# Token routing of a two-FFN transformer block: paired token sums, statistics three batches ahead, a new order on ScalarE

## The reference, cut to what matters

```python
x = x + 0.5 * ffn(layernorm(x))          # first FFN
x = x + attn(layernorm(x))
x = x + 0.5 * ffn(layernorm(x))          # second FFN
# in ffn, per batch, S = 64 slots:
h = gelu(concat(x, slot_mean) @ w1 + b1)                  # 128 hidden
route_logits = (h @ w2 + b2) / (abs(tau) + 0.1)           # 64 logits a token
topk_vals, topk_idx = top_k(route_logits, 8)
alpha = scatter(softmax(topk_vals))                       # weights, zero off the top 8
slot_input = einsum('bts,btd->bsd', alpha, x)
si = slot_input / (alpha.sum(axis=1) + 1e-8)
# then a GRU cell, slot attention, layernorm, and out = alpha @ slot_values @ wo + bo
```

## Time and profile before

| what | value |
|---|---|
| time, median of 3 runs (lowest, highest) | 3647.28 us (3645.79, 3649.57) |
| the profiled execution | 3644.44 us |
| its span | 3642.4 us |
| mean granted TensorE clock | 0.973 |
| busy: PE / DVE / ACT / POOL | 94% / 84% / 75% / 28% |
| routing, first FFN | 17.88 to 239.1 us |
| routing, second FFN | 3274.7 to 3495.5 us |

### The profile page before, as it was taken

How to read it: one execution, slowest core, us unless ns; L and a number is a source line. 1 busy time by engine, 2 the same in 40 slices (tenths; PEclk the granted TensorE clock), 3 DMA queues, 4 the chain that set the end, 5 groups by cost and what they waited for, 6 DMA issues and landing times. The chain is left out here.

```text
span 3642.4 us, 60476 instructions
## 1 busy us (share of the span) xinstructions
PE 3420.0 (94%) x22538; PEld 1210.3 (33%) x22538; DVE 3065.4 (84%) x4480; ACT 2722.1 (75%) x5316; POOL 1023.3 (28%) x835
## 2 busy tenths in 40 slices
PE   6998489999999999999999999999999999958987
PEld 4644212232322323232323232323232232215653
DVE  6965499999999999999999999999999989808965
ACT  4740158888888888888888888888888888856730
POOL 2320323232323232333333342323232321212310
PEclk8999679999999999999999999999999999988999
DMA  3225302121212121121212121112121212112217
GB/s 103 93 94 214 141 22 54 43 54 43 54 43 62 43 57 43 54 60 41 64 43 60 41 63 44 54 42 54 43 60 44 59 31 54 40 52 77 93 71 300
DMA packets 123093, 246.53 MB, mean 68 GB/s; under 512 B 34657, under 2 KB 75425, under 8 KB 108465
## 3 DMA queue, kind: packets, MB, share of 16 engines
q1 hardware_dynamic: 115712, 208.06, 20.5%
q10 hardware_dynamic: 7088, 34.61, 2.3%
HBM read 121.91 MB, written 51.38 MB: 48 GB/s over the span
## 5 line engine op out<-in xcount | busy, mean ns | idle before, releaser
L1360 DVE TENSOR_REDUCE attn_part_max<-attn_ps 128x2 f32<-128x1024 f32 x2048 | 2447.3, 1221 | 244.7 <-PE attn_ps L1500 202.7
L1625 ACT ACTIVATE attn_probs<-attn_ps 128x512 f32<-128x512 f32 x4096 | 2171.1, 600 | 363.1 <-PE attn_ps L1512 362.7
L1512 PE MATMUL attn_ps<-attn_q_rows,attn_k_rows 50*128 50x512 f16 x4096 | 1273.0, 384 | 29.4 <-ACT attn_probs L1625 16.1
L1500 PE MATMUL attn_ps<-attn_k_rows,attn_q_rows 48*128 48x512 f16 x4096 | 1140.2, 388 | 30.2 <-DVE attn_part_max L1360 26.6
L1526 PE MATMUL attn_ps<-attn_probs,attn_v_ones 128*32 128x512 f32 x8192 | 1091.8, 605 | 0.7 <-ACT attn_probs L1625 0.7
L1512 PEld LDWEIGHTS attn_ps<-attn_q_rows,attn_k_rows 50*128 50x128 f16 x4096 | 307.3, 94 | 1324.8 <-ACT attn_probs L1625 1249.6
L1500 PEld LDWEIGHTS attn_ps<-attn_k_rows,attn_q_rows 48*128 48x128 f16 x4096 | 225.4, 94 | 174.0 <-DVE attn_part_max L1360 159.4
L1526 PEld LDWEIGHTS attn_ps<-attn_probs,attn_v_ones 128*32 128x32 f32 x8192 | 161.1, 108 | 237.4 <-issue 136.8
L1452 PE MATMUL attn_ps<-attn_xn_parts,attn_w_qk 128*128 128x256 f16 x1536 | 214.3, 278 | 6.2 <-POOL attn_xn_parts L1284 6.2
L1247 POOL CAST attn_max_parts<-attn_max_whole 32x128 f16<-32x128 f32 x64 | 17.9, 279 | 687.8 <-ACT attn_max_whole L1577 666.6
L1272 POOL TENSOR_TENSOR attn_xn_t<-attn_o_packed,attn_inv_wide 128x1024 f32<-128x1024 f32 x32 | 75.4, 2357 | 397.5 <-DMA attn_inv_wide<-inverse_denominators 397.5
(11 more groups left out here) (170 smaller groups left out, 2649.7 us busy)
## 6 DMA issues: line engine op xcount, KB each, us to landing
attn_q_rows<-attn_parts SPq DMA_DIRECT2D x384, 64.0 KB, 2.2
attn_k_rows<-attn_parts SPq DMA_DIRECT2D x384, 64.0 KB, 2.2
ffn_x_ring<-in_L_attn_x SPq DMA_DIRECT2D x16, 1024.0 KB, 5.7
attn_x_ln<-after_first_ffn SPq DMA_DIRECT2D x16, 1024.0 KB, 4.8
attn_o_packed<-attn_o_sb SPq DMA_DIRECT2D x256, 64.0 KB, 2.3
attn_inv_wide<-inverse_denominators SPq DMA_DIRECT2D x32, 512.0 KB
attn_x_res<-after_first_ffn SPq DMA_DIRECT2D x16, 1024.0 KB, 5.1
after_attention<-attn_x_res SPq DMA_DIRECT2D x16, 1024.0 KB, 8.6
```

Source lines behind the costliest of these rows:

```text
L1360: dve.tensor_reduce(part_max[:, G % 2, :, j, t, half], pair, AX.X, ALU.max).then_inc(dve_emptied, 1)
L1500: last = pe.matmul(ps[:, bank + e, :], q_rows[rows_e, G % NG, j, t * P:(t + 1) * P], k_rows[rows_e, G % NG, j, half * HALF:(half + 1) * HA ...
L1512: pe.matmul(ps[:, bank, :], k_rows[rows_e, G % NG, h // 2, kt * P:(kt + 1) * P], q_rows[rows_e, G % NG, h // 2, half * HALF:(half + 1) * H ...
L1625: act.activation(probs[:, quad % NQ, h, :], bank_of(s, b0), ACT.Exp, scale=1.0 / (SCALE * SCALE)).then_inc(act_emptied, 1)
```

## The change

Only the routing block is changed.

- The ring has 8 places. SyncE loads eight batches at once, and batch b from 8 on once pair (b-8)//2 has been summed.
- `sum_tokens` works on a pair of batches: in each step four token tiles, for each tile the even batch and right behind it the odd one. A pair is summed in the steps 2p+3 (tiles 0 to 3) and 2p+4 (tiles 4 to 7).
- TensorE's step n is now `hidden(n)`, fills 0 and 1 of batch n+1, `logits(n)`, fills 2 and 3 of batch n+1, `turn_sums` (odd steps), half of a pair's sums, `turn_weights` (odd steps).
- VectorE's step n is `find_top(n)`, `normalise(n+2)`, `statistics(n+3)`, `weigh(n)`, and `divide` in even steps. The shift is no longer made by VectorE: it makes the negated mean, and GpSimd multiplies it with rstd right behind `rsqrt`.
- The total of the eight weights comes from eight extra columns: GpSimd appends the top 8 logits less the largest to `shifted`, Exp takes 72 columns a tile instead of 64, and VectorE adds up 8 of them instead of the 64 picked ones.
- ScalarE's step n is Exp of batch n-1, Gelu of n, fills 0 and 1 of n+1, then in even steps `normalise(n+2)`, fills 2 and 3, `alpha_t`, in odd steps fills 2 and 3, `si_t`, `normalise(n+2)`.
- mean, rstd and shift have two buffers.

```diff
-    R = 4
+    R = 8
...
+            STEPS = B + 5
...
+                for b in range(B):
+                    if b >= R:
+                        sp.wait_ge(si_ready, (b - R) // 2 + 1)
+                    sp.dma_start(x_ring[:, b % R, :, 0:D], rows(x_in, b)).then_inc(x_loaded[b % R], 16)
...
                 def rsqrt(b):
+
                     pool.wait_ge(var_ready, b + 1)
...
+                    if b >= 2:
+                        pool.wait_ge(xn_low, b - 1)
+                        pool.wait_ge(xn_high, b - 1)
+                    pool.tensor_tensor(rstd[:, b % 2, :], var_eps[:, :], c.neg_half[:, 0:TT], ALU.pow).then_inc(rstd_ready, 1)
+                    pool.wait_ge(rstd_ready, b + 1)
+                    pool.tensor_tensor(shift[:, b % 2, :], neg_mean[:, :], rstd[:, b % 2, :], ALU.mult).then_inc(shift_set, 1)
 
                 def less_largest(b):
                     pool.wait_ge(top_step, b * (2 * TT) + TT)
...
+                    pool.tensor_tensor(shifted[:, :, 0:S], logit[:, :, :], top8[:, :, 0:1].to_broadcast([P, TT, S]),
                                        ALU.subtract).then_inc(shift_ready, 1)
...
+                    pool.tensor_tensor(shifted[:, :, S:S + 8], top8[:, :, :], top8[:, :, 0:1].to_broadcast([P, TT, 8]),
+                                       ALU.subtract).then_inc(shift_ready, 1)
...
+                rsqrt(1)
+                rsqrt(2)
+                for n in range(B):
+                    less_largest(n)
+                    if n + 3 < B:
+                        rsqrt(n + 3)
+                    scale(n)
...
+                    dve.tensor_scalar(neg_mean[:, :], mean_var[:, b % 2, :, 0], -1.0, None, ALU.mult)
...
-                    dve.scalar_tensor_tensor(shift[:, :], mean_var[:, :, 0], -1.0, rstd[:, :], ALU.mult,
-                                             ALU.mult).then_inc(shift_set, 1)
...
+                    dve.tensor_reduce(total[:, :], expd[:, :, S:S + 8], AX.X, ALU.add).then_inc(pick_step, 1)
+                    dve.scalar_tensor_tensor(picked[:, :, :], rest[:, :, :], NEG, expd[:, :, 0:S], ALU.is_equal,
                                              ALU.mult).then_inc(pick_step, 1)
                     dve.wait_ge(pick_step, b * 3 + 1)
-                    dve.tensor_reduce(total[:, :], picked[:, :, :], AX.X, ALU.add).then_inc(pick_step, 1)
-                    dve.wait_ge(pick_step, b * 3 + 2)
                     dve.reciprocal(inv_total[:, :], total[:, :]).then_inc(pick_step, 1)
...
+                    if n < B:
+                        find_top(n)
+                    if n + 2 < B:
+                        normalise(n + 2)
+                    if n + 3 < B:
+                        statistics(n + 3)
+                    if n < B:
+                        weigh(n)
+                    if n % 2 == 0 and 4 <= n <= B + 2:
+                        divide((n - 4) // 2)
...
                     for t in tiles:
...
+                        for e in range(2):
+                            last = pe.matmul(ps_si[e * S:(e + 1) * S, 0:D + 1], alpha[:, pair % 2, t, e, :], x_ring[:, (2 * pair + e) % R, t, :],
+                                             start=(t == 0), stop=(t == TT - 1), skip_group_check=True)
...
+                for n in range(STEPS):
+                    pair, first = (n - 3) // 2, 0 if n % 2 else TT // 2
+                    summing = 0 <= pair < PAIRS
                     if n < B:
+                        hidden(n)
+                    if n + 1 < B:
+                        turn_rows(n + 1, (0, 1))
                     if n < B:
+                        logits(n)
+                    if n + 1 < B:
+                        turn_rows(n + 1, (2, 3))
+                    if n % 2 and 5 <= n <= B + 3:
+                        turn_sums((n - 5) // 2)
+                    if summing:
+                        sum_tokens(pair, range(first, first + TT // 2))
+                    if n % 2 and summing:
+                        turn_weights(pair)
...
+                    if 1 <= n <= B:
+                        weights(n - 1)
...
                     if n + 1 < B:
+                        take_rows(n + 1, (0, 1))
+                    if n % 2 == 0 and n + 2 < B:
+                        normalise(n + 2)
+                    if n + 1 < B:
+                        take_rows(n + 1, (2, 3))
...
+                    if n % 2 and n + 2 < B:
+                        normalise(n + 2)
```

More of the change, by code:

```diff
@@ L357, in _ @@
                 rsqrt(0)
-                def step(b, q, r, n):
-                    if 1 <= n <= B:
-                        less_largest(b - 1)
-                    if n + 1 < B:
-                        pool.wait_ge(xn_high, b + 1)
-                        rsqrt(b + 1)
-                    if 1 <= n <= B:
-                        scale(b - 1, q * (R // 2) + (r - 1) // 2, (r - 1) % R, n - 1)
-                over_batches(pool, step)
+                rsqrt(1)
[5 more added lines that the diff above has]
+                    scale(n)
@@ L427, in divide @@
                     dve.reciprocal(den_inv[:, :], den_eps[:, :]).then_inc(den_step, 1)
-                    dve.wait_ge(den_step, pairs * 2)
-                    if n >= 5:
-                        dve.wait_ge(si_turned, pairs - 1)
+                    dve.wait_ge(den_step, 2 * pair + 2)
+                    if pair >= 1:
+                        dve.wait_ge(si_turned, pair)
                     dve.tensor_scalar(si_rows[:, :], ps_si[:, 0:D], den_inv[:, 0:1], None, ALU.mult).then_inc(si_taken, 1)
-                statistics(0, 0)
@@ L434, in _ @@
-                normalise(0, 0)
-                def step(b, q, r, n):
-                    if 1 <= n <= B:
-                        find_top(b - 1)
-                    if n + 1 < B:
-                        statistics(b + 1, (r + 1) % R)
-                    if 1 <= n <= B:
-                        weigh(b - 1, n - 1)
-                    if n + 1 < B:
-                        normalise(b + 1, (r + 1) % R)
-                    if n % 2 and 3 <= n <= B + 1:
-                        divide(pairs_of(q, r), n)
@@ L447, in _ @@
-                over_batches(dve, step)
+                statistics(0)
+                normalise(0)
+                statistics(1)
+                normalise(1)
+                statistics(2)
+                for n in range(STEPS):
[9 more added lines that the diff above has]
+                        divide((n - 4) // 2)
@@ L449, in _, with turn_rows @@
             @block.tensor
             def _(pe):
[L451 removed]
+                def turn_rows(b, fills):
                     for f in fills:
@@ L521, in step @@
                     if n < B:
-                        turn_rows(b, r, n, (2, 3))
-                    sums(1, 2, 3)
-                    if n < B:
-                        hidden(b, n)
-                    if n % 2 == 0 and n >= 4:
-                        turn_sums(pairs_of(q, r))
-                    sums(4, 5, 6, 7)
-                    if n % 2 and 3 <= n <= B + 1:
-                        turn_weights(pairs_of(q, r), r, n)
-                    if n < B:
-                        logits(b, n)
@@ L539, in normalise @@
+                def normalise(b):
                     act.wait_ge(shift_set, b + 1)
                     for t in range(LOW, TT):
-                        last = act.activation(x_ring[:, r, t, 0:D], x_ring[:, r, t, 0:D], ACT.Identity,
-                                              bias=shift[:, t:t + 1], scale=rstd[:, t:t + 1])
+                        last = act.activation(x_ring[:, b % R, t, 0:D], x_ring[:, b % R, t, 0:D], ACT.Identity,
+                                              bias=shift[:, b % 2, t:t + 1], scale=rstd[:, b % 2, t:t + 1])
@@ new lines, in weights @@
+                def weights(b):
+                    act.wait_ge(shift_ready, 2 * b + 2)
+                    if b >= 1:
+                        act.wait_ge(pick_step, 3 * (b - 1) + 2)
+                    act.activation(expd[:, :, :], shifted[:, :, :], ACT.Exp).then_inc(exp_done, 1)
+                normalise(0)
+                take_rows(0, (0, 1, 2, 3))
+                normalise(1)
+                for n in range(STEPS):
+                    if 1 <= n <= B:
+                        weights(n - 1)
+                    if n < B:
+                        act.wait_ge(hid_ready, n + 1)
```

149 lines of the change are left out of this document (62 added, 87 removed).

## The result

| | median | lowest to highest | runs |
|---|---|---|---|
| before | 3648.43 us | 3645.79 to 3667.14 | 4 |
| after | 3600.16 us | 3598.87 to 3601.52 | 4 |

The ratio is 0.9866, with an interval of 0.9843 to 0.9888: 48 us, or 1.3%, faster. The profiled execution took 3598.87 us against 3644.44, 45.6 less.

The account below looks back on a forecast made before the run. VectorE and TensorE were both taken as close to the bound in the routing blocks. Per block 22.8 us gained in the steps, 1.3 lost, 1.7 gained: 23.2, 46.4 for two, hence 3601 us, range 3586 to 3624.

Parts of the forecast that it names:

- 15 steps, gain in a block: Routing block's steady steps: each falls from 12.17 to 10.65 us, 22.8 us gained a block.
- end shorter: Block's end: last logits follow the Gelu at once, 1.5 us gained, and shorter weigh, 0.2: 1.7 us.
- shift; extra difference on GpSimd: GpSimd's step: the new shift on 8 columns and the new difference of 64 elements, 0.3 us each.
- The pairs: TensorE's sums: two column halves run beside each other, so 16 instructions take 1.95 us, not 3.76.
- TensorE's own step: TensorE's work from hidden through half a pair's sums: 9.77 us in even steps, 11.02 in odd, 20.8 for two.
- The loop: Logits, find_top, normalising, statistics, rsqrt, shift, ScalarE's normalising, fills, hidden, Gelu, logits: 21.1 us for two steps, taken as 21.3.
- neither is met in full: Margin in two steps: TensorE's 20.8 us and the loop's 21.1 lie so near that 21.3 was taken.
- The start: Block's start: ScalarE normalises batch 1 ahead of the first Gelu, with rstd late; 0 to 2.1 us lost, 1.3 taken.
- Loads: Eight loads at once, batch 8 asked for over 11 us before it is read: cost nothing.
- Rival A: TensorE's paired sums run one behind the other: 12.2 us a step, nothing gained there, 3653 us; chance 0.05.
- Rivals B and C: VectorE and GpSimd disturb each other: in part (B), 3624 us, chance 0.10; in full (C), slower, 3683 us, chance 0.06.

Follow-up runs that it names:

- The halves apart: Kernel after, with a half pair's eight sums for the even batch first, then the eight for the odd one, not alternating: 3619.15 us, ratio 0.9932.
- statistics-first kernel: Kernel after, with VectorE's order find_top without MATCH_REPLACE, statistics, normalising, MATCH_REPLACE, weigh: median 3592.41 us, ratio 0.9843.
- late MATCH_REPLACE: Kernel after, with VectorE's eight MATCH_REPLACE moved out of find_top to behind the statistics, just ahead of weigh: 3593.99 us, ratio 0.9848.

## Why the prediction was right, step by step

3601 was predicted and 3600.2 measured; of the sum's 46.4 us, 45.6 came. The mechanism is the predicted one, but the closeness is partly luck. The fifteen steps come out at 15 x 10.69 only because the fourth Gelu's 3.0 us at the lower clock are made up by a first step of 8.80 and a last of 9.61, which the sum had at the full price. And the start, with a term of 1.3, was 2.7 later in one block and 0.5 earlier in the other.

| step | predicted | measured |
|---|---|---|
| sums, 16 instructions | 1.95 us | 1.90 |
| TensorE's own two steps | 20.8 | 20.3 |
| loop between the engines, two steps | 21.1, taken 21.3 | 21.38 |
| 15 steps, gain in a block | 22.8 | 22.2 and 22.0 |
| first Gelu later | 1.3 | 2.7 and -0.5 |
| end shorter | 1.7 | 1.5 |
| shift; extra difference on GpSimd | 0.3; 0.3 | 0.20; 0.29 |

*The pairs.* Right in size: the quarters of the attention were a good pattern for halves. The halves apart show that the alternating order is a real part of this, worth 19 us.

*TensorE's own step* was 0.5 too big. The statistics-first kernel, where nothing else holds it, gives 9.61 and 10.66 us against 9.77 and 11.02. The fills hold TensorE 0.88 to 0.97 us from start to start, not the printed 1.09, and `hidden` behind the turned weights leads to its Gelu after 3.64, not 3.74. Printed durations were used where starts should have been.

*The loop.* The mechanism is shown: a shorter rsqrt, or earlier statistics, frees TensorE's 20.3. Its terms, predicted and measured: `find_top` to rsqrt 8.6 and 8.47; rsqrt and shift 2.28 and 2.45; shift to Gelu 7.04 and 7.25; Gelu 1.16 and 1.17; `logits` 2.00 and 2.03. Two were off. Rsqrt took 2.13, not 1.98, starting beside the picked weights. And the way from shift to Gelu was worked out through TensorE. By that way the Gelu could have started at 116.80 (`hidden` at 113.06, and 3.74). But ScalarE's own queue is longer: normalising, fills, `alpha_t`, a table load, Exp and another table load, from 109.97 to 117.22. The prediction called Exp covered; its table loads and `alpha_t` are 0.4 us on the path. Of the margin of 0.2 taken because "neither is met in full", this is the real content.

*The start.* This is the term that was mis-sized, 1.3 us for ScalarE's normalising of batch 1 ahead of the first Gelu. In this trace that normalising costs nothing: it waits for rstd as predicted, but it and the table load are over at 39.76, and the Gelu waits until 41.25 for `hidden`, at the lower clock. Where the first `hidden` of the first block ran at the full clock, as it did before, the Gelu does come right behind ScalarE's table load, 21.4 us into the block in the kernel run once more and 21.6 to 21.8 in five of the experiments with the same start, against 20.7 before: 0.7 to 1.1. Where both were at the lower clock, in the second block, nothing is lost. So the term is worth at most 1.1, and the rest of the 2.7 is the level that this execution happened to meet.

The fourth Gelu lost 3 more, inside the fifteen steps, and that did come with the change. The prediction knew the clock only as a mean; it did not ask what the engine is granted where sums are missing. It also took the 20.7 us before the first Gelu from the first block for both, while the second had 23.4, with `hidden` at the lower clock.

*Loads* cost nothing that shows: the first statistics wait 6.60 us for data against 6.32 before.

*Rival A*, pairs in a row: out, by 1.90 us. *Rivals B and C*, VectorE and GpSimd in each other's way: out here, with the picked weights at 0.68 beside rsqrt and normalising at 1.38. But B's price is real, as the late MATCH_REPLACE shows. It stayed away because `less_largest` (111.62, 1.06 us) and the extra difference end at 112.92, and normalising starts at 113.14: a reserve of 0.2 us.

## What to carry to other kernels

When two engines are both near the bound, relieving one brings little (9 of 48 us here), so work out both steps and then the loop that closes over all engines, through each engine's own queue. After the change look for the wait that is left: here it named the next gain, some 17 us in the two blocks, from reordering VectorE's work alone. Where a stage starts or an order leaves TensorE waiting, look at the granted clock of that stretch before believing a term measured at the full one; and count from where a block begins, not from the start of the trace, before calling its first instruction late.

## What the runs showed of the hardware

- Two column halves of TensorE in turn: 16 float32 instructions of 257 columns in 1.90 us; the same in two runs of eight: 2.81; one batch at a time in the kernel before: 3.76.
- The lower clock level came in stretches with waits of 1.2 to 2.3 us for ScalarE, and at the fourth `hidden` it went when unread matmuls filled them; it cost 2 to 3 us on one `hidden`. A wait alone does not tell: behind 2.36 or 2.37 us the second `hidden` took 6.77 in the kernel after run once more and 3.70 with statistics first. The first `hidden` was at either level in executions of one kernel.
- Eight float32 instructions in one half, then eight in the other, overlap where they meet: five or six are at work in a window of 0.2 us there, two or three at both ends.
- rsqrt on GpSimd, 128x8: 1.64 us beside MATCH_REPLACE, 1.73 beside normalising, 2.13 where it starts 0.04 us behind the picked weights (1.98 at 0.21 behind them, and 1.64 where it starts 0.33 ahead of them). The picked weights took 0.68 or 0.69 in every case.
- A product of 128x8 on GpSimd: 0.20 us alone, 0.73 beside the picked weights. Normalising on VectorE: 1.38, and 2.11 beside a difference of 512 elements on GpSimd.
